# First units of the second FFN issued among the last weighted sums of an attention kernel

## The reference, cut to what matters

```
x = x + 0.5 * ffn(layernorm(x))
x = x + attn(layernorm(x))
x = x + 0.5 * ffn(layernorm(x))        # same weights as the first

attn:  q, k, v = x Wq', x Wk', x Wv';   softmax(q k') / sqrt(128) @ v
ffn:   shared = silu(x @ Ws_up) @ Ws_down
       aff = x @ centroids'             # 64 experts
       idx = top 8 of aff + expert_biases
       w   = sigmoid(aff[idx]), divided by its sum (+1e-8)
       cw  = w scattered over the 64 experts
       routed = sum over e of cw[:, e] * (silu(x @ W_up[e]) @ W_down[e])
       return shared + routed
```

## Time and profile before

| what | value |
|---|---|
| median of 3 runs | 545.74 us (545.43 to 548.09) |
| the profiled execution's own time | 545.78 us |
| its span, first to last instruction | 544.0 us |
| TensorE matmul busy | 533.0 us, 98% of the span |
| TensorE weight loads busy | 435.0 us, 80% |
| VectorE, ScalarE, GpSimd busy | 407.0, 407.3, 274.0 us |
| granted TensorE clock | 1.000 |
| chain that ended last | TensorE 88%, VectorE 6%, ScalarE 2%, issue 2%, DMA 1% |

### The profile page before, as it was taken

One profiled execution on the slowest core, in us unless ns is written; L12 is line 12 of the kernel. 1 busy time (PEld: TensorE's weight loads), 2 busy tenths in 40 slices (PEclk: granted clock), 3 DMA queues, 4 the chain that ended last, 5 costly groups with the idle time before them and its releaser, 6 DMA issues.

```text
span 544.0 us, 8636 instructions
## 1 busy us (share of the span) xinstructions
PE 533.0 (98%) x2679; PEld 435.0 (80%) x2679; DVE 407.0 (75%) x926; ACT 407.3 (75%) x814; POOL 274.0 (50%) x242
## 2 busy tenths in 40 slices
PE   8899999999999999999999999999999999999997
PEld 5577887887888887699999999777887888788885
DVE  5989679877976676767777889778677867866564
ACT  6899778877887776766666667678778777877774
POOL 3579767775776763000000000166675776766663
PEclk9999999999999999999999999999999999999999
DMA  7676565554565540000000000055555565656562
GB/s 259 182 215 194 184 195 161 179 189 159 173 187 196 189 157 1 1 1 1 1 2 1 1 1 1 16 195 168 174 202 159 175 194 179 176 166 201 198 189 92
DMA packets 44270, 72.25 MB, mean 133 GB/s; under 512 B 8864, under 2 KB 9632, under 8 KB 44224
## 3 DMA queue, kind: packets, MB, share of 16 engines
q1 hardware_dynamic: 43568, 71.17, 41.9%
q10 hardware_dynamic: 592, 0.39, 0.2%
q0 software_dynamic: 64, 0.13, 0.1%
HBM read 69.57 MB, written 2.10 MB: 132 GB/s over the span
## 4 chain that ended last, share of the span: by engine, by line
PE 88%; DVE 6%; ACT 2%; issue 2%; DMA 1%; SPq 0%; DVEq 0%
PE lrow L1064 13%; PE lrow L1065 13%; PE lrow L1066 13%; PE bank L1102 11%; PE bank L1104 11%; PE bank L1103 11%; PE bank L1136 6%; PE bank L1348 3%; PE bank L1350 2%; PE bank L1349 2%; DVE pmax L879 1%; PE bank L1143 1%; PE bank L1064 1%; PE bank L1065 1%; PE bank L1066 1%
## 5 line engine op out<-in xcount | busy, mean ns | idle before, releaser
L277 POOL TENSOR_TENSOR gpart_lo<-gated,gpart_hi 128x512 fp32r<-128x512 f32 x174 | 224.0, 1296 | 164.2 <-ACT gpart_hi L442 162.5
L431 ACT ACTIVATE lrow<-lrow 128x512 f32<-128x512 f32 (+1 forms) x246 | 144.4, 587 | 63.9 <-PE lrow L1066 63.5
L678 DVE TENSOR_TENSOR gated<-lrow,wide 128x512 f32<-128x512 f32 x170 | 116.3, 684 | 57.6 <-ACT lrow L431 56.3
L442 ACT CAST gpart_hi<-gated 128x512 fp32r<-128x512 f32 x174 | 106.7, 613 | 5.7 <-DVE gated L678 5.1
L1102 PE MATMUL bank<-gpart_lo,wdn_hi 128*128 128x512 f32 x256 | 101.7, 397 | 0.0
L1104 PE MATMUL bank<-gpart_hi,wdn_hi 128*128 128x512 f32 x256 | 101.4, 396 | 0.0
L1103 PE MATMUL bank<-gpart_hi,wdn_lo 128*128 128x512 f32 x256 | 101.1, 395 | 0.0
L678 DVE TENSOR_TENSOR lrow<-lrow,wide 128x512 f32<-128x512 f32 x74 | 51.5, 696 | 28.0 <-ACT lrow L431 28.0
L997 DVE TENSOR_TENSOR pT_lo<-bank,pT_hi 128x512 fp32r<-128x512 f32 x64 | 43.8, 685 | 24.2 <-ACT pT_hi L618 24.2
L277 DVE TENSOR_TENSOR gpart_lo<-lrow,gpart_hi 128x512 fp32r<-128x512 f32 (+1 forms) x84 | 57.3, 682 | 1.8 <-ACT gpart_hi L442 1.3
L1102 PEld LDWEIGHTS bank<-gpart_lo,wdn_hi 128*128 128x128 f32 x256 | 48.0, 188 | 11.8
(11 more groups left out here) (246 smaller groups left out, 944.2 us busy)
## 6 DMA issues: line engine op xcount, KB each, us to landing
wide<-gates_dram SPq DMA_DIRECT2D x488, 128.0 KB, 3.0
raw<-in_w_up SPq DMA_DIRECT2D x8, 256.0 KB, 6.1
raw<-in_w_down SPq DMA_DIRECT2D x8, 256.0 KB, 6.3
gates_dram<-gates SPq DMA_DIRECT2D x8, 128.0 KB, 2.3
x<-in_x SPq DMA_DIRECT2D x3, 256.0 KB, 3.7
out_dram<-x SPq DMA_DIRECT2D x3, 256.0 KB, 3.0
x<-in_x SPq DMA_DIRECT2D x1, 128.0 KB, 2.7
x<-in_x ACTq DMA_DIRECT2D x1, 128.0 KB, 2.9
```

The costliest lines, as they stand in the source:

```text
L277: return eng.tensor_tensor(gpart[1][0:m, U % NGP, :], gated_at(U)[0:m, :], gpart[0][0:m, U % NGP, :].bitcast(F32), ALU.subtract)
L431: nc.scalar.activation(dst[0:m, :], hid[U % NH][0:m, :], ACT.Silu).then_inc(s_silu, 1)
L442: nc.scalar.copy(gpart[0][0:m, U % NGP, :], gated_at(U)[0:m, :]).then_inc(s_ghi, 1)
L678: nc.vector.tensor_tensor(gated_at(U), a, b, ALU.mult).then_inc(s_gated, 1)
```

## The change

The number of ups before the loop goes from four to seven (`LEADS`), so that the loop starts with unit 7 on TensorE; ups 0 to 3 are issued between turn_p(15, 3) and the rest of the weighted sums, the transposes of the expert weights within these sums, and spreads 1 to 6, ups 4 to 6 and downs 0 and 1 follow in an order written out. Spreads 2 and 4 write bank 2 (the one that held the turned weights) and wait for the copy of the gates in place of `a_x`; the wait on `a_x` moves to spread 6. The silu of unit 0 goes to a slot of `wide`. `o_copy(6)` and `lo_o(6)` stand before the last tile's last turn. `inverse(7)` comes before the last add. VectorE's stats of chunk 5 move ahead of gate 1. ScalarE and VectorE get the same early units written out.

```diff
-LEADS = (4, 4)
+LEADS = (4, 7)
+        def gate_bank(u, n):
+            return bank[2][:, :] if n == NCH and u in (2, 4) else gate[(u + 1) % 2]
...
@@ gated_at
+            if U == place(0, NCH):
+                return wide[:, slot_of(EARLY, NCH), :]
...
@@ silu_unit (ScalarE)
-                dst = hid[U % NH]
+                dst = hid[U % NH] if u or n == 0 else gated_at(U)
...
+                if n == NCH and u == EARLY:
+                    wait_low(act, place(0, n))
...
@@ ScalarE, loop of a chunk
-                    for u in range(min(c, 1), UNITS):
+                    for u in range(7 if n == NCH else min(c, 1), UNITS):
@@ ScalarE, last tiles
                         turn_hi(t, 2)
+                        if t == NT - 1:
+                            o_copy(NQ - 2)
                         turn_hi(t, 3)
                     pro_sil(NCH)
-                    o_copy(NQ - 2)
+                    for u in range(4):
+                        silu_unit(u, NCH)
                     make_sel()
+                    pro_cwT(NCH)
                     o_copy(NQ - 1)
-                    for u in range(2):
-                        silu_unit(u, NCH)
-                    pro_cwT(NCH)
-                    for u in range(2, LEADS[1]):
-                        silu_unit(u, NCH)
+                    hi_unit(0, NCH)
+                    silu_unit(4, NCH)
+                    hi_unit(1, NCH)
+                    silu_unit(5, NCH)
+                    hi_unit(2, NCH)
+                    hi_unit(3, NCH)
+                    silu_unit(6, NCH)
+                    hi_unit(4, NCH)
+                    hi_unit(5, NCH)
@@ gate_unit (VectorE)
-                    a, b = g, gate[(u + 1) % 2]
+                    a, b = g, gate_bank(u, n)
@@ normed (VectorE)
+                    if n == NCH + 1:
+                        dve.wait_ge(s_gated, nth_gated(4, NCH))
@@ VectorE, loop of a chunk
-                    for u in range(min(c, 1), UNITS):
+                    for u in range(5 if n == NCH else min(c, 1), UNITS):
...
-                            if u == 2:
+                            if n != NCH and u == 2:
                                 stats(0, c + 1, p_st, (2, 3))
@@ add_o (VectorE)
-                        inverse(g)
+                        if g < NQ - 1:
+                            inverse(g)
@@ VectorE, last tiles
+                        if j == 2:
+                            lo_o(NQ - 2)
-                    lo_o(NQ - 2)
                     chosen(NCH)
                     first_weights(NCH)
+                    inverse(NQ - 1)
                     add_o(NQ - 2)
+                    stats(0, 1, p_st)
+                    gate_unit(1, NCH)
                     lo_o(NQ - 1)
+                    lo_unit(0, NCH)
+                    gate_unit(2, NCH)
+                    gate_unit(3, NCH)
                     add_o(NQ - 1)
+                    gate_unit(4, NCH)
+                    lo_unit(3, NCH)
@@ up (TensorE)
-                if U >= NH:
+                if n == NCH and NH <= u < LEADS[1]:
+                    pe.wait_ge(s_silu, U - NH + 1)
+                elif U >= NH:
                     wait_hid_free(pe, U - NH)
@@ spread_gate (TensorE)
                     if u == 2 and n:
+                        pe.wait_ge(s_gates, NCH + 1)
+                    if u == EARLY and n:
                         pe.wait_ge(a_x, NQ)
@@ TensorE, loop of a chunk
-                    for u in range(min(c, 1), UNITS):
+                    for u in range(LEADS[1] if n == NCH else min(c, 1), UNITS):
@@ TensorE, last tiles
                     turn_p(NT - 1, 3)
-                    weigh(NQ - 1, range(4, NT))
+                    for u in range(4):
+                        up(u, NCH)
+                    weigh(NQ - 1, range(4, 8))
                     turn_o(NQ - 2)
-                    for u in range(2):
-                        up(u, NCH)
+                    weigh(NQ - 1, range(8, 11))
+                    pro_cw(NCH)
+                    weigh(NQ - 1, range(11, NT))
+                    pe.wait_ge(p_cwr, 2)
+                    spread_gate(1, NCH)
+                    spread_gate(2, NCH)
+                    up(4, NCH)
+                    up(5, NCH)
                     turn_o(NQ - 1)
-                    pro_cw(NCH)
-                    for u in range(2, LEADS[1]):
-                        up(u, NCH)
+                    spread_gate(3, NCH)
+                    down(0, NCH)
+                    up(6, NCH)
+                    spread_gate(4, NCH)
+                    down(1, NCH)
+                    spread_gate(5, NCH)
+                    spread_gate(6, NCH)
```

More of the change, by code:

```diff
@@ L1086, in spread_gate @@
                     if u == 2 and n:
+                        pe.wait_ge(s_gates, NCH + 1)
+                    if u == EARLY and n:
                         pe.wait_ge(a_x, NQ)
                     one = sel[:, u - 1, :, :].rearrange("p e f -> p (e f)")
-                    nc.tensor.matmul(gate[(u + 1) % 2], one, cwT[:, :], start=True, stop=True).then_inc(s_gate, 1)
+                    nc.tensor.matmul(gate_bank(u, n), one, cwT[:, :], start=True, stop=True).then_inc(s_gate, 1)
             def down(u, n):
```

## The result

The changed kernel takes 544.19 us (median of 11 runs, 543.82 to 546.08) against 545.43 us for the kernel before on the same chips: 1.24 us less, a ratio of 0.9968 with a 95% interval of 0.9954 to 0.9982. (The quotient of the two medians is 0.9977, that of the means 0.9965.) Three of the eleven executions of the kernel before (548.09 to 548.25) and one of the changed kernel (546.08) lie 2 to 3 us above most others of their kernel, and without these four the medians are 545.38 and 544.10, 1.28 apart. The forecast was 544.3, within 543.3 to 545.7, and no difference above 0.5%. The profiled execution spans 542.1 us against 544.0.

What follows compares the result with a forecast made beforehand. TensorE's matmul work stays the same, so only its standing time can be won: 2.87 us before, 0.50 + 0.07 + 0.50 + 0.34 = 1.41 after, 1.46 less. From 545.78 that gives 544.3 us, range 543.3 to 545.7.

Steps and rivals of the forecast that it cites:

- The ceiling: TensorE's standing time from 344.73 to 356.89, summed wait by wait: 2.87 us, of which 2.37 winnable.
- the matmul column: Busy-time reading of the 12.2 us handover: 12.20 - 10.83 = 1.37 us idle, the ceiling if matmul busy time were right.
- more matmuls than 52: Sign of being right: the 12 us of the handover would hold more matmuls than the 52 of before.
- TensorE up to up 6: From the last turn's transposes on: expert weights covered by 1.2 us; waits of 0.45, 0.82 and 0.60 gone.
- The shape of down(0): down(0) contracts 64 partitions between products of 128: 0.50 us that moves with it and stays.
- Up 7: VectorE sets the pace: spread 6 waits 0.07 for gate 4, up 7 waits 0.40 for unit 3's low part, restart 0.10.
- Up 10: VectorE's queue of 5.53 us from gate 4 ends unit 6's low part at 359.21: wait 0.24, restart 0.10.
- The sum: Standing after the change 0.50 + 0.07 + 0.50 + 0.34 = 1.41 against 2.87: 1.46 us less, 544.3 us.
- the third rival: The late root: chunk 5's norm waits for its root on GpSimd, up 10 starts 1.8 later: 546.2 us; chance 0.1.
- All of it goes: Rival: low parts 3 and 6 come before TensorE wants them, 2.37 us go: 543.4 us; chance 0.15.
- Eaten lead: Rival: VectorE loses another us before unit 6's low part, up 10 waits that long: 545.3 us; chance 0.2.

Runs made afterwards that it cites:

- experiment 4: Changed kernel with unit 0 of chunk 4 taken over 128 rows in place of 64, for timing only: profile 26.74 us, median 544.12 us, ratio 0.9972.
- Experiment 2: Changed kernel with ups 0 to 3 behind all weighted sums again: profile 28.72 us, median 545.68 us, ratio to before 0.9999.
- Experiment 3: Changed kernel with unit 3's low part ahead of gate 4 on VectorE: profile 26.83 us, median 544.15 us, ratio to before 0.9976.
- Experiment 6: Three unused statistics instructions added on VectorE before chunk 5's norm, in both kernels: profile 27.67 us (changed), 28.57 us (before).
- experiment 8: Changed kernel with unit 0 of chunk 4 in joint form, down 0 as two matmuls over 128 partitions: profile 26.85 us, median 544.05 us, ratio 0.9982.
- experiment 9: Changed kernel with both unit 0 in joint form and unit 3's low part ahead of gate 4: profile 26.84 us, median 543.75 us, ratio 0.9964.
- experiment 7: Changed kernel with gates 2 and 4 in bank 1 again, spread 2 waiting for the last add to x: profile 28.96 us, median 546.07 us, ratio 0.9999.
- two versions here: Changed kernel with chunk 5's norm later (544.36 us); that with low part 3 first, joint unit 0 and the steps after the norm one unit later (544.45 us).
- the last experiment: The changed kernel itself run again, unaltered: profile 27.12 us, median 544.30 us against 545.57 us before, ratio 0.9978.
- experiment 10: Changed kernel with low part 3 first, joint unit 0, and chunk 5's norm and its following steps one unit later: median 544.45 us, ratio 0.9979.

## Why the prediction was right

**The ceiling.** The standing time, 2.87 us with 2.37 of it winnable, was read from the starts of matmuls and not from the busy time. The runs bear that out: 1.46 came, and 1.82 in experiment 4 (28.56 - 26.74), both more than the 1.37 us of the matmul column. The weight loads after the change can't confirm it, as their share depends on the columns of the matmuls (all of the time among those of 256, 9.70 of 12.20 us in the undisturbed stretch of 512). The forecast's sign of "more matmuls than 52" has the same weakness.

**TensorE up to up 6.** No wait up to down(0), as forecast. The expert weights are ready 1.28 us before TensorE takes them (344.65 and 345.93), where the forecast had 1.2 of cover. Experiment 2 shows what makes it: without the 2.8 us of ups in front, TensorE waits 1.54.

**The shape of down(0).** The sign and the place were right, the size was not: 0.44 in the changed kernel, 0.39 of it the shape (experiment 4), in place of 0.50. In the kernel before, spread 4 came behind a wait, and its step of 0.43 held a restart, which the term took in.

**Up 7.** Forecast 0.07 before spread 6 and 0.40 + 0.10 before up 7, together 0.57; measured 0.58 and a step 0.07 longer, 0.65. Experiment 3 shows that unit 3's low part is what it waited for.

**Up 10.** The queue behind gate 4 was forecast at 5.53 us and took 5.52 (353.19 to 358.71). Where TensorE stands for it was wrong in part: I had 0.24 + 0.10 at up 10, and it is 0.13 at the turn of the norm and 0.10 at up 10, 0.23 in place of 0.34. I overlooked that the turn waits for all four tiles of the norm at once. It stands in front of up 9, so it took the wait over. Experiment 6 shows that the cover on VectorE is spent: 0.59 us more cost 0.57 now, and nothing before.

**The sum, and what was luck.** The standing time left was forecast at 0.50 + 0.57 + 0.34 = 1.41 and measured at 0.44 + 0.65 + 0.23, with 0.07 in other small steps, 1.39. The terms missed by up to 0.11, in both directions; that the gain agrees to the last digit is luck. So is part of the 544.3: it was reckoned from 545.78, and from the 545.43 of the kernel before beside the changed one the same 1.46 give 543.97, where 544.19 was measured. The medians say 1.24 and can't tell this from 1.46. And 1.8 us above the forecast is 546.1, not the 546.2 of the third rival.

**The rivals.** All of it goes: no, VectorE holds the rest. Eaten lead: the 0.3 to 1 us more of VectorE that it needed did not come; experiment 6 is that case in small. The late root: it decided nothing in the changed kernel (0.46 of cover, forecast 0.4), but with the old banks it did, and it is the next bound in experiments 8 and 9. So the banks, with the order that they allow, are a needed part of the change, and so is the place of the ups; the casts and the inverse alone are not worth anything. That the bank and the ups each seem to bring all of the gain is no contradiction: each hides a wait that by itself takes it back.

**What stays open.** Whether the version with low part 3 first and unit 0 in the joint form is faster than the changed kernel: 0.26 us in the profile are too few for these medians. Not tried by themselves: the earlier statistics of chunk 5 and the silu of unit 0 in `wide`. And experiment 7 changes the banks and, since the old bank waits for the last add, the order of spreads and gates with them; what the bank does in the new order is not shown.

## What to carry to other kernels

Where one engine sets the time, add up the steps between the starts of its instructions over their undisturbed length; that sum is the ceiling of any reordering. Name for each part what it waits for, or the shape that costs it. A lead given to that engine is worth only what the next queue can follow, so walk that queue too, from the last thing it must wait for to the first thing that is waited for. And after moving a step, look far enough behind it: two versions here won 0.3 and 0.8 us at first and gave them back at 24 and 43 us behind the last turn.

## What the runs showed of the hardware

**The clock.** In the profile of the last experiment TensorE ran at half its clock for some 6 us near the start (from about 20 to 26.5 us), in the same code that ran at full clock in the changed kernel's first profile. The same stretch in both, the changed kernel first (us; busy time of PE, PEld, DVE, ACT, POOL; granted clock; DMA share; GB/s), then the repeat with a few of its rows:

```profile
21.00:28.00 7.00, 6.98 (x32) 5.16 (x31) 6.48 (x16) 5.72 (x11) 3.43 (x3) 1.00 0.81 243
```

```profile
21.00:28.00 7.00, 7.00 (x19) 5.06 (x19) 5.36 (x15) 3.71 (x8) 2.56 (x2) 0.59 0.80 246
...
19.87 0.76 PE L1121 MATMUL bank<-cwT,sel 128*128 128x512 f32 x1 [0.37 <-DVE lrow L694]
...
24.44 0.63 PE L1135 MATMUL bank<-gpart_hi,wdn_lo 128*128 128x512 f32 x1
24.87 0.63 PE L1136 MATMUL bank<-gpart_hi,wdn_hi 128*128 128x512 f32 x1
...
26.57 0.49 PE L1092 MATMUL lrow<-xnT_lo_a,wup_hi 128*128 128x512 f32 x1
```

A matmul of 512 columns steps by 0.43 us there and by 0.23 at full clock, the 1.2 and 2.4 GHz levels. In front of it TensorE had been busy 5.06 us from 0 to 7, 5.55 from 7 to 14 and 3.95 from 14 to 19 in the changed kernel's first profile, and 5.45, 5.41 and 3.94 in the repeat, and one fell and the other did not. The last turn starts 2.7 us later in the repeat, at 342.26, and the execution took 546.61 us. In the profile of experiment 8 the clock fell too, at another place, from about 9 to 15.7 us, and the last turn there starts at 341.63. Most kernels have some executions about this far above the rest, the one before too (548.1 to 548.3); experiments 9 and 10 have none. So in the two executions whose profiles show it, the extra time lies in the first 27 us and says nothing of the change.

**Rows.** A change between 128 and 64 contracted partitions costs TensorE 0.39 us there and back around three matmuls of 512 columns (experiment 4). A joint form of 128 rows avoids it (experiment 8, steps of 0.27, 0.24, 0.23 and 0.23 from the spread on). But there VectorE's instruction that reads partitions 64 to 127 and writes 0 to 63 took 0.69 us and the next one started 0.72 after it, behind its end (351.84 and 352.56, the same in experiments 9 and 10); in the changed kernel, where it reads and writes partitions 0 to 63, that step is 0.59.
